# Moving one activation-table load and swapping two VectorE steps in a fused attention and expert-layer kernel

## The reference

```python
xn = layernorm(x)
qkv = xn @ Wqkv
# 1. fast weights: 4 heads of 64, in chunks of 128 tokens, each chunk changes W0, W1, W2
q, k = l2norm(silu(q)), l2norm(silu(k));  v = silu(v)
lr = softplus(xn @ Wlr + c);  mom = sigmoid(xn @ Wm + bm)
out = (silu(q W0') * (q W2')) W1'                  # with the weights before this chunk
dw0, dw1, dw2 = gradients(k, v, lr) + M * mean(mom)
dw = newtonschulz5(dw)                              # 5 rounds of A = X X'; B = bA + cAA; X = aX + BX
W = rownorm(W + dw) * n                             # carried to the next chunk
# 2. sliding-window attention: 2 heads of 128, window 128 (this block and the one before)
p = softmax(mask(aq ak' / sqrt(128)));  att = p av
# 3. expert layer: 32 experts of 128, 8 chosen by sigmoid scores and groups, and a shared part
h = relu(xl w1[e]')**2;  y = sum_e cw[e] * (h w2[e]');  shared = relu(xn up')**2 down'
result = x + (rms(out) * silu(xn @ Ws + bs) + att) @ Wo + shared + y @ fc2'
```

## Time and profile before

| what | value |
| --- | --- |
| median of 3 runs | 781.8 us |
| the profiled execution's own time | 781.77 us |
| its span, first to last instruction | 780.0 us |
| its mean granted clock of TensorE | 0.995 |
| busy: TensorE, VectorE, ScalarE, GpSimd | 95%, 78%, 59%, 24% of the span |
| one body of the loop | 48.19 us |

### The profile page before, as it was taken

One profiled execution on the slowest core, in us unless ns is written; L12 is line 12 of the kernel. 1 busy time (PEld: TensorE's weight loads), 2 busy tenths in 40 slices (PEclk: granted clock), 3 DMA queues, 4 the chain that ended last, 5 costly groups with the idle time before them and its releaser, 6 DMA issues. The chain is left out here.

```text
span 780.0 us, 24469 instructions
## 1 busy us (share of the span) xinstructions
PE 743.6 (95%) x9776; PEld 639.5 (82%) x9776; DVE 611.4 (78%) x2448; ACT 461.9 (59%) x1146; POOL 184.5 (24%) x257
## 2 busy tenths in 40 slices
PE   4899999999999999999999999999999999999997
PEld 2878789787887888878788797887978889788886
DVE  4778878787887878878688786877878878797766
ACT  1765566655666656666566655566556665655654
POOL 1412223122231222312222122320223203222020
PEclk9899999999999999999999999999999999999999
DMA  8200000000000000000000000000000000000000
GB/s 315 76 9 14 11 3 18 6 15 10 2 22 2 16 8 2 22 2 16 8 3 21 2 15 9 3 21 3 16 8 2 23 2 16 8 3 15 2 16 8
DMA packets 9809, 15.07 MB, mean 19 GB/s; under 512 B 1120, under 2 KB 8928, under 8 KB 9440
## 3 DMA queue, kind: packets, MB, share of 16 engines
q1 hardware_dynamic: 7904, 7.80, 3.4%
q10 hardware_dynamic: 1792, 5.70, 1.8%
HBM read 11.41 MB, written 2.10 MB: 17 GB/s over the span
## 5 line engine op out<-in xcount | busy, mean ns | idle before, releaser
L1332 DVE SCALAR_TENSOR_TENSOR acc<-YB,cw,acc 128x128 f32<-128x128 f32 x448 | 125.6, 343 | 54.2 <-PE YB L630 54.0
L630 PE MATMUL YB<-e_s,hq 128*128 128x128 f32 x1024 | 141.2, 281 | 2.7 <-DVE acc L1332 1.0
L630 PE MATMUL HB<-xlT,e_s 128*128 128x128 f32 x1024 | 143.3, 284 | 0.4 <-ACT xlT L415 0.4
L300 POOL TENSOR_TENSOR r<-r,half 128x3 f32<-128x3 f32 (+1 forms) x78 | 77.9, 1011 | 265.4 <-DVE r L1021 159.1
L630 PEld LDWEIGHTS HB<-xlT,e_s 128*128 128x128 f32 x1024 | 127.0, 193 | 6.8 <-ACT xlT L415 0.7
L630 PEld LDWEIGHTS YB<-e_s,hq 128*128 128x128 f32 x1024 | 124.1, 191 | 8.5 <-issue 5.3
L415 ACT ACTIVATE hq<-HB 128x512 f32<-128x512 f32 x128 | 76.3, 596 | 77.8 <-PE HB L630 77.8
L415 ACT ACTIVATE hq<-hq 128x512 f32<-128x512 f32 x128 | 80.7, 630 | 4.0
L415 ACT ACTIVATE XT<-CC 128x256 f32<-128x256 f32 x150 | 48.8, 376 | 26.9 <-PE CC L701 26.9
L630 PEld LDWEIGHTS CC<-X,Mp 64*64 64x64 f32 x1800 | 45.5, 133 | 21.6 <-DVE Mp L1150 10.6
L630 PEld LDWEIGHTS CC<-XT 64*64 64x64 f32 x1800 | 42.6, 133 | 24.7 <-ACT XT L415 20.8
(11 more groups left out here) (181 smaller groups left out, 1460.2 us busy)
## 6 DMA issues: line engine op xcount, KB each, us to landing
xa<-in_x SPq DMA_DIRECT2D x16, 128.0 KB, 2.1
e_s<-in_e1T ACTq DMA_DIRECT2D x1, 2048.0 KB, 12.9
e_s<-in_e2T ACTq DMA_DIRECT2D x1, 2048.0 KB, 19.3
xr<-in_x SPq DMA_DIRECT2D x16, 128.0 KB, 2.2
out<-ot SPq DMA_DIRECT2D x16, 128.0 KB, 1.7
wall<-in_wall SPq DMA_DIRECT2D x1, 820.0 KB, 6.7
up_s<-in_upT ACTq DMA_DIRECT2D x1, 512.0 KB, 14.7
down_s<-in_downT ACTq DMA_DIRECT2D x1, 512.0 KB, 20.0
```

Source lines behind the costliest of these rows:

```text
L300: return pool.tensor_tensor(dst, src, expo[:, 0:n], ALU.pow)
L630: return pe.matmul(out_, lhsT, rhs, start=start, stop=stop)
L1332: ins = nc.vector.scalar_tensor_tensor(acc[:, e, :], y, w, acc[:, e, :], ALU.mult, ALU.add)
```

## The change

Two lines of the `fill` tables change. On ScalarE, `to_sigmoid` is called in stage 15 behind `probs_T`, and no longer in stage 19 behind `x_lat`. On VectorE, `prep_ss8` moves from stage 9 to stage 8, and `y_acc(i, 3)` from stage 8 to stage 9. A `fill` entry runs behind the Newton-Schulz instructions of its stage. So VectorE's order was `prep_silu_v`, `y_acc 3`, `ns_a` (both groups), `prep_ss8`, `prep_mean`, and is now `prep_silu_v`, `prep_ss8`, `ns_a` (both groups), `y_acc 3`, `prep_mean`. No instruction is added or removed, and all waits inside the functions stay.

```diff
@@ block.scalar, body @@
-                        13: [lambda: probs(i)], 14: [lambda: h_relu(i, 7), lambda: lr_ln(m)], 15: [lambda: probs_T(i)],
-                        18: [lambda: comb_T(i)], 19: [lambda: x_lat(m), to_sigmoid]}
+                        13: [lambda: probs(i)], 14: [lambda: h_relu(i, 7), lambda: lr_ln(m)], 15: [lambda: probs_T(i), to_sigmoid],
+                        18: [lambda: comb_T(i)], 19: [lambda: x_lat(m)]}
@@ block.vector, body @@
-                        8: [lambda: prep_silu_v(m), lambda: y_acc(i, 3)], 9: [lambda: prep_ss8(m), lambda: prep_mean(m)],
+                        8: [lambda: prep_silu_v(m), lambda: prep_ss8(m)], 9: [lambda: y_acc(i, 3), lambda: prep_mean(m)],
```

## The result

The changed kernel takes 794.06 us (median of 4 runs, 792.43 to 794.57), the kernel before 781.78 us (4 runs). The ratio is 1.0161, with a 95% interval of 1.0148 to 1.0172: 1.6% slower. Forecast were 794.0 us and a range of 785.5 to 797.5.

A forecast was written before the change was run, and what follows sets the result against it. TensorE, busy 95% of the span, was taken as the bound. Delays from VectorE's order and the load, meeting on ScalarE, cost 0.83 us in each of 15 bodies, 12.4 us: 794.0 us forecast, range 785.5 to 797.5.

The forecast's parts named there:

- The load taken out of stage 19: ScalarE behind xlT: without the load it idles 2.3 us and starts the relu at the same moment; gain 0.
- The load in stage 15: ScalarE between prT and XT: XT 0.80 us late, att_pv covers most, stage 17's gram on TensorE 0.20 late.
- nothing is added: Stage 17: group 1's XT and gram come 0.3 us behind group 0's, so the load's cost stays 0.2 a body.
- The sum waits for the squares: VectorE, stages 8 to 10: prep_ss8 waits until 342.38, so prep_qkn and Mp come 0.27 us later.
- y_down 4 0.63 late: TensorE waits for y_acc 3; the 0.35 us Mp wait swallows part, leaving stage 15 0.3 us late.
- The meeting on ScalarE: Late h_up 7 delays relu 7 and prT, the load fills the idle time behind; gram 0.83 us late a body.
- The rule on the drain: Skill's rule of 2.66 us per table switch, some 815 us in all; rejected for the trace's 1.3 us.
- A: Rival: costs stay apart, prT on ScalarE only 0.27 us late, 0.47 a body, 788.8 us; chance 0.17.
- B: Rival: load hidden in stage 15, only VectorE's 0.27 us a body left, 785.8 us; chance 0.06.
- C: Rival: more than forecast; milder, nothing swallowed at stage 15, some 800 us; other, switch holds ScalarE 2.56 us, 813; chance 0.07.
- E: Rival: nothing measurable, y_down 4 does not wait for y_acc 3 and the load lies in idle time; chance 0.04.
- D: Rival: earlier sum brings prep_qkn and Mp forward, TensorE's 0.35 us wait goes, 776.5 us; chance 0.04.

The follow-up runs named there:

- e4: The changed kernel with the table load one stage later, in stage 16 behind the XT copies: 786.32 us.
- e2: The kernel before with only VectorE's order changed, the load staying in stage 19: 785.48 us.
- e1: The kernel before with only the table load moved to stage 15, VectorE's order unchanged: 789.98 us.
- e9: The changed kernel, with GpSimd's products kl and vl also waiting for comb: 793.55 us.
- e3: The kernel before with VectorE's sum (prep_ss8) moved behind y_acc 3 and ahead of ns_a, load in stage 19: 775.47 us.
- e8: The kernel before with VectorE's order ns_a, y_acc 3, prep_ss8, prep_mean, load in stage 19: 795.26 us.
- e7: The kernel before with VectorE's order ns_a, prep_ss8, y_acc 3, prep_mean, load in stage 19: 781.93 us.
- e10: The kernel before with VectorE's order ns_a, prep_ss8, y_acc 3, prep_mean, load in stage 15, kl and vl waiting for comb: 790.31 us.
- e5: The kernel before with only the load moved to stage 15, and kl and vl waiting for comb: 785.51 us.

## Why the prediction was right, step by step

- **The load taken out of stage 19 gains nothing.** Right: 2.34 us of idle, forecast 2.3; e4 and e2 agree with the load in two different free places.
- **The load in stage 15, XT 0.80 late, gram 0.20 late.** Right for these two (e1: 0.23). "Alone, this edit costs 0.2 us a body" was wrong: e1 costs 0.58. The step that failed is "nothing is added": I followed the delay of the gram on TensorE and did not ask what VectorE and GpSimd would be doing at the same moment once VectorE is 0.2 late. In the changed kernel this term costs nothing but in body 9: comb takes 565 ns on average there, kl has 0.92 us of lead, TensorE has no wait at its turn, and e9 without any collision is as slow as the changed kernel. The prediction has nothing on kl and comb, so it is luck that the changed kernel, with its longer delay, passes by the collision.
- **The sum waits for the squares, prep_qkn 0.27 late.** Right to 0.01 us, with some luck: the mean cost 0.35 and not 0.30, y_acc 1.03 and not 1.05, lr_a 0.07 and not 0.10, and these cancel. The chain by which it matters (sum, power, prep_qkn, Mp of stage 14) is shown from both sides by e3, 0.42 earlier and 0.41 gained, and e8, 0.91 later and 0.92 lost.
- **y_down 4 0.63 late, of which 0.3 stays at stage 15.** Right: 0.62 and 0.26. e7 shows the swallowing by itself.
- **The meeting on ScalarE, 0.83 in all.** Right: 0.83 a body, 0.79 of it at the start of the gram; e9 and e10 isolate 0.3 of it. The busy 2.28 of 2.31 us of ScalarE from the relu to prT, which the prediction takes from rows 2, does not stand there. It is the fourth busy time of this row of the kernel before:

```profile
351.30:353.61 2.31, 2.00 (x36) 1.91 (x37) 1.78 (x12) 2.28 (x7) 0.00 (x0) 1.00 0.04 7
```

- **The rule on the drain.** In the changed kernel XT starts at 360.13, 0.02 us behind the load's end (358.83 + 1.28 = 360.11), and the load 0.01 behind the end of prT: 1.31 us in all. The 2.66 us that the Trainium skill gives for a switch (page "ScalarE: Activation LUTs", section "What ACT_TABLE_LOAD costs") does not show in this kernel, even with a waiting instruction right behind.
- **The rivals.** A, the costs stay apart, is the one that two runs could have made believable: e1 and e2 cost 0.58 and 0.28, which adds up to 0.86, as if they were independent. This is chance. The collision in e1 (0.32) is about as large as the meeting on ScalarE (0.3), and each occurs where the other does not. e5 and e9 tell them apart. A's own condition, that prT is only 0.27 late, fails too: it is 0.57 late. B is refuted by e1 and e5. C's milder form is refuted by stage 15, 0.26 late and not 0.6, its other form by the 1.31 us above, and E by y_down 4's wait. D needed the sum earlier without y_acc 3 late; the change does not do this, e3 does.

The version to keep is e3: 775.5 us, 0.75% faster than before.

## What to carry to other kernels

In a loop whose bottleneck engine waits in several places, price a delay at each engine separately: the bottleneck may swallow it at its next wait, while a helper engine that was released by the delayed piece carries it on to where it has no pause left. Put a step without inputs, such as a table load, behind the instruction that others wait for, not into the short pause ahead of it. And two single-edit runs that add up to the whole do not show that the edits are independent.

## What the runs showed of the hardware

Comb is a VectorE addition, 128x256, with both inputs in SBUF, the on-chip memory that the engines share. It took 425 ns in e5, where no GpSimd product runs beside it. It took 870 ns at one place of e1, where it started just after one of GpSimd's products, 0.19 us later in relation to them than in the kernel before, and it ended 0.28 us after that product. The Trainium skill (page "SBUF — State Buffer", section "Who interferes with whom") has the rule: a VectorE instruction with two inputs in SBUF and a GpSimd instruction that reads SBUF exclude each other, and the first to be issued wins. The traces agree on both sides: comb first, the kl pair took 1.38 us; a kl product first, the pair took 1.20 and comb waited. A shift of 0.2 us in the schedule thus cost 0.3 us a body.

The exclusion is not seen over the whole length of a row. In the kernel before, comb starts at 308.72, while the first product runs until about 308.90, and yet it takes only 0.48 us. If comb always needs 0.425 us of its own, an estimate from e5, it began that work about 0.13 us ahead of the recorded end of the product in the kernel before, and 0.15 ahead of it in e1.
